# Layer 0's gated MLP rewritten: four batches wide, the weights stationary, every product as three float32r products on split halves, the down products issued two tiles later

## The chip, the cores and the metric

One core of a Trainium2 chip runs the whole program. The metric is the device time in microseconds, the median of several executions. PE is the matrix engine (PEld its weight loads), DVE the vector engine, ACT the scalar engine, POOL the general one, SP the engine that issues the DMAs.

## What is computed

Two decoder layers on x of 16 batches x 128 tokens x 256, each with self attention, cross attention and a gated MLP, each behind a layernorm. The change lies in the MLP of layer 0:

```python
def _mlp(x, gw, uw, dw):
    g = x @ gw.T
    u = x @ uw.T
    return g * jax.nn.sigmoid(g) * u @ dw.T
logits = x @ router_weight.T                      # 8 experts
topk_vals, topk_idx = jax.lax.top_k(logits, 2)
comb_w = jnp.sum(jax.nn.softmax(topk_vals) * (topk_idx < 8), axis=-1)
shared = _mlp(x, sh_gate, sh_up, sh_down)         # inner width 1024
routed = _mlp(x, r_gate, r_up, r_down)            # inner width 128
x = x_in + shared + routed * comb_w[:, None]      # x here is layernorm(x_in)
```

## The kernel before

x stays in SBUF for the whole program, 128 tokens on the partitions, 256 columns per batch. The program is a chain of blocks, one per sublayer, and each block has one instruction stream per engine, written out by hand and tied by semaphores; no scheduler moves anything. All engines finish a block before the next begins. Each block loads the next one's weights by DMA.

`gated_mlp` is the block in question. It takes one batch per turn in a software pipeline (`pipeline`: four steps written out, then a loop of two). For batch t: DVE normalises x into h (`dve_normalise`), PE transposes h (`pe_transpose_h`), ACT copies it out of PSUM (`act_copy_hT`), and PE multiplies. The activations are the moving side with 128 columns (one batch) and the weights the stationary side, in plain f32 (L1629). The three parts of a batch are the routed expert with the router (L1639) and two halves of four inner tiles. For each part ACT computes tanh(g/2) (L1545), DVE forms (tanh+1) * g (L1570) and multiplies by u (L1575). In the next turn PE multiplies by the down weights (L1617, L1621), here with the inner activations stationary and 256 weight columns moving. DVE then adds both results to x (L1594, L1596) and takes the statistics for the next layernorm (`dve_statistics`, L169 to L173); POOL raises the variance to the power -1/2 (`pool_rstd`, L134).

The first cross attention (`normed_cross_attention`) already multiplies in float32r: a value is split in a high part (its float32r rounding) and a low part (the rest), and three products of the parts (`PARTS`: high x high, high x low, low x high) stand for one f32 product.

## Time and profile before

| | |
|---|---|
| median of 3 runs | 1830.47 us (1828.85 to 1833.53) |
| the profiled execution, its own time | 1829.69 us |
| its span, first to last instruction | 1827.7 us |
| busy: PE, DVE, ACT, POOL | 92%, 62%, 42%, 38% of the span |
| mean granted clock of PE | 0.979 of full speed |
| the gated MLP's block, by its instructions | about 702 to 910 us |

An engine is busy where one of its instructions runs. Idle time matters on the engine that bounds a stage, and there the profile names what ended it. [...]

### The profile page before, as it was taken

What the parts mean: (1) busy time and instruction counts of PE and PEld (TensorE: products, weight loads), DVE (VectorE), ACT (ScalarE), POOL (GpSimd) and SP (SyncE); (2) the same over time, 40 slices, a digit from 0 to 9 for tenths busy, and PEclk for the clock granted to TensorE, in tenths of its full rate; (3) what the DMA queues carried; (4) which work ended last, traced back from release to release, by engine and by line L of the source; (5) the groups of instructions that cost most, each with busy time, mean ns of one, the idle gap of its engine ahead of it and who ended that gap; (6) DMA issues with size and microseconds to landing.
All of it is one profiled execution on the core that took longest, in us unless ns stands there. A gap on an engine that the chain in (4) does not pass through costs nothing. (4 is left out here: it accounts for less than half of the span.)

```text
span 1827.7 us, 33438 instructions
## 1 busy us (share of the span) xinstructions
PE 1681.9 (92%) x10800; PEld 1283.1 (70%) x10800; DVE 1129.3 (62%) x2543; ACT 771.2 (42%) x1771; POOL 691.5 (38%) x884
## 2 busy tenths in 40 slices
PE   4999889999999998999878888899999999888887
PEld 2555568888888887999845555588888888644444
DVE  3666557677676663554445666445556555499996
ACT  1444346767676762111134444344444444311111
POOL 3666535454545541000012222023333322366665
PEclk9999989999999999999979999999999999999999
DMA  5000020000000000000020000200000000000000
GB/s 210 1 0 0 1 81 4 3 3 3 1 3 3 1 2 20 1 0 0 2 114 0 0 0 0 76 6 7 6 6 6 6 3 5 0 7 10 10 9 11
DMA packets 15631, 28.41 MB, mean 16 GB/s; under 512 B 1745, under 2 KB 12242, under 8 KB 14802
## 3 DMA queue, kind: packets, MB, share of 16 engines
q1 hardware_dynamic: 15570, 27.63, 4.1%
q8 instruction: 34, 0.56, 0.1%
q14 instruction: 27, 0.22, 0.0%
HBM read 25.53 MB, written 2.10 MB: 15 GB/s over the span
## 5 line engine op out<-in xcount | busy, mean ns | idle before, releaser
L1237 POOL TENSOR_TENSOR weights_even<-weights_even,cross_reciprocal 128x512 f32<-128x512 f32 x64 | 66.7, 1043 | 283.2 <-DVE cross_reciprocal L1341 283.2
L134 POOL TENSOR_TENSOR rstd<-variance,minus_half 128x1 f32 (+1 forms) x80 | 43.9, 549 | 336.1 <-DVE variance L173 336.1
L844 POOL TENSOR_TENSOR weights_odd<-weights_odd,cross_reciprocal 128x512 f32<-128x512 f32 x64 | 66.5, 1040 | 191.6 <-DVE cross_reciprocal L970 191.6
L1629 PE MATMUL bank<-mlp_hT,weights_even 128*128 128x128 f32 x1152 | 136.5, 278 | 0.5 <-ACT mlp_hT L152 0.5
L1629 PEld LDWEIGHTS bank<-mlp_hT,weights_even 128*128 128x128 f32 x1152 | 133.6, 193 | 1.5 <-ACT mlp_hT L152 0.8
L1420 PE MATMUL bank<-cross_hT,cross_wqk 128*128 128x128 f32 x1024 | 124.9, 275 | 0.6 <-ACT cross_hT L1267 0.6
L1033 PEld LDWEIGHTS bank<-ident,weights_odd 128*128 128x128 f32 x768 | 94.1, 141 | 44.4 <-issue 32.4
L1101 PE MATMUL bank<-weights_odd 128*128 128x256 f32 x512 | 121.5, 380 | 1.6 <-ACT weights_odd L900 1.6
L1453 PE MATMUL bank<-weights_even 128*128 128x256 f32 x512 | 121.2, 380 | 0.7 <-ACT weights_even L1291 0.7
L1420 PEld LDWEIGHTS bank<-cross_hT,cross_wqk 128*128 128x128 f32 x1024 | 119.5, 192 | 0.9 <-ACT cross_hT L1267 0.9
L1033 PE MATMUL bank<-ident,weights_odd 128*128 128x128 f32 x768 | 115.5, 273 | 2.2 <-DVE weights_odd L956 2.2
L1848 DVE TENSOR_REDUCE grouped_maxima<-bank 128x4 bf16<-128x512 f32 x128 | 82.3, 685 | 56.5 <-PE bank L1914 56.4
L2216 PE MATMUL bank<-weights_even,mx_hT 128*128 128x512 f32 x256 | 115.2, 593 | 1.1 <-ACT mx_hT L152 1.1
L1279 ACT ACTIVATE weights_even<-bank,cross_shift 128x128 f32<-128x128 f32 x256 | 73.0, 368 | 74.3 <-DVE cross_shift L1331 73.7
L1762 ACT ACTIVATE grouped_probs<-bank 128x512 f32<-128x512 f32 x128 | 67.6, 600 | 85.9 <-PE bank L1932 85.9
L1101 PEld LDWEIGHTS bank<-weights_odd 128*128 128x128 f32 x512 | 92.3, 190 | 13.6 <-ACT weights_odd L900 3.5
L1453 PEld LDWEIGHTS bank<-weights_even 128*128 128x128 f32 x512 | 92.3, 190 | 11.4 <-ACT weights_even L1291 1.5
L883 ACT ACTIVATE weights_odd<-bank,cross_shift,cross_q_rms 128x128 f32<-128x128 f32 x256 | 95.9, 457 | 2.6 <-DVE cross_shift L950 2.6
L1329 DVE TENSOR_REDUCE cross_maxima<-bank 128x4 f32<-128x512 f32 x64 | 44.2, 691 | 78.7 <-PE bank L1430 78.6
L1336 DVE TENSOR_REDUCE cross_sums<-weights_even 128x4 f32<-128x512 f32 x64 | 43.9, 686 | 77.3 <-ACT weights_even L1279 77.3
L368 POOL TENSOR_TENSOR causal_masked_maxima<-causal_maxima,causal_constants 128x512 bf16<-128x512 bf16 x64 | 67.7, 1079 | 60.6 <-DVE causal_maxima L493 60.6
L1047 PE MATMUL bank<-high_weights,cross_high 128*128 128x512 f32 x192 | 87.5, 456 | 1.2 <-DVE cross_low L979 1.2
(264 smaller groups left out, 4029.7 us busy)
## 6 DMA issues: line engine op xcount, KB each, us to landing
weights_odd<-in_weights SPq DMA_DIRECT2D x2, 3072.0 KB, 14.0
weights_even<-in_weights SPq DMA_DIRECT2D x2, 2560.0 KB, 11.7
weights_even<-in_weights SPq DMA_DIRECT2D x2, 1732.0 KB, 8.7
weights_odd<-in_weights SPq DMA_DIRECT2D x2, 1536.0 KB, 8.7
x<-in_x SPq DMA_DIRECT2D x4, 512.0 KB, 7.1
cross_context<-in_context SPq DMA_DIRECT2D x32, 64.0 KB, 1.8
out<-mx_result SPq DMA_DIRECT2D x16, 128.0 KB, 1.7
weights_even<-in_weights SPq DMA_DIRECT2D x2, 512.0 KB, 9.0
```

The lines of the kernel that those rows point to most:

```text
L368: pool.tensor_tensor(masked_maxima[g][:, :, :], maxima[s][:, g, :].unsqueeze(2).to_broadcast([P, PER, P]), later.unsqueeze(1).to_broadcast ...
L883: last = act.activation(probs[x][:, j, :], bank_scores[:, j * P:(j + 1) * P], ACT.Exp, scale=q_rms[x][:, j:j + 1], bias=shift[x][:, j:j + 1])
L1033: last = pe.transpose(bank[:, j * P:(j + 1) * P], source, core.ident[:, :])
L1047: last = pe.matmul(out, half[:, c, :], split_weights[b][:, at:at + PER * D], start=(k == 0), stop=(k == len(jobs) - 1))
L1101: last = pe.matmul(bank_y[:, 0:EMBED], headsT[x][:, j, :], wo[:, h, :], start=(h == 0), stop=(h == HEADS - 1))
L1279: last = act.activation(probs[x][:, j, :], bank_scores[x][:, j * P:(j + 1) * P], ACT.Exp, scale=SCALE, bias=shift[x][:, j:j + 1])
L1420: last = pe.matmul(bank_q[:, j * P:(j + 1) * P], wqk[:, c, h * D:(h + 1) * D], hT[s][:, c, :], start=(c == 0), stop=(c == EC - 1))
L1453: last = pe.matmul(bank_y[s][:, 0:EMBED], headsT[x][:, j, :], wo[:, h, :], start=(h == 0), stop=(h == HEADS - 1))
L1629: last = pe.matmul(out, wt[:, c, m * P:(m + 1) * P], layer.hT[:, c, :], start=(c == 0), stop=(c == EC - 1))
L1762: act.activation(probs[:, SLOTS * c + j, :], bank_scoresT[j][:, :], ACT.Exp, scale=SCALE)\
L1848: dve.tensor_reduce(maxima[s][:, g * PER:(g + 1) * PER], bank_scores[j].rearrange("p (h k) -> p h k", h=PER), AX.X, ALU.max).then_inc(max_ ...
L2216: last = pe.matmul(bank[:, :], layer.hT[:, c, :], wt[:, c, j * 512:(j + 1) * 512], start=(c == 0), stop=(c == EC - 1))
```

## The change

`gated_mlp` now takes a quad, four batches (512 token columns), at a time. The routed expert is tile 0 of nine inner tiles of 128; per tile the packed weights hold gate, up and down side by side (`by_inner_tile` on the host), and the router's 16 columns come last. All products are float32r: ACT writes the high parts of the weights, of h transposed and of the inner activations, DVE the low parts of the weights and of h, POOL the low part of the inner activations. Gate and up have the weights stationary and 512 columns moving, in two pairs of banks that alternate. Down has the inner activations of one batch stationary and 256 weight columns moving; the downs of a tile are issued behind the gate and up of the tile two later, or behind the quad's last tile. The whole block is written out, without a loop. The odd weight area, 12288 columns wide, exists only up to the cross attention; a new one of 6144 columns serves the blocks from `gated_mlp` on. The cut diff (the removed code is that of the functions above):

```diff
-    HALVES = 2
-    PER = TILES // HALVES
+    INTER, EXPERTS = 1024, 8
+    TILES = INTER // P + 1
+    QUAD = 4
+    QUADS = BATCHES // QUAD
+    LAST = TILES - 1
+    PER_TILE = 2 * EC * P + EMBED
+    ROUTER_AT = TILES * PER_TILE
+    COLUMNS = ROUTER_AT + EC * EXPERTS
...
+        split_weights = [sbuf(f"{name}_weights", [P, COLUMNS], F32R) for name in ("high", "low")]
+        h = sbuf("all_h", [P, QUAD, EMBED])
+        hT = [sbuf(f"{name}_hT", [P, EC, QUAD * P], F32R) for name in ("high", "low")]
...
+        halves = [[sbuf(f"{name}_inner{s}", [P, QUAD * P], F32R) for name in ("high", "low")] for s in range(2)]
...
+        bank_h, bank_y = core.banks[0:2], core.banks[6:8]
+        bank_gate, bank_up = [core.banks[2], core.banks[4]], [core.banks[3], core.banks[5]]
...
+            def low_inner(i):
+                pool.wait_ge(inner_high, i + 1)
+                pool.wait_ge(tile_down, downs(i - 2))
+                pool.tensor_tensor(halves[i % 2][1][:, :], inner[i % 2][:, :],
+                                   halves[i % 2][0][:, :].bitcast(F32), ALU.subtract).then_inc(inner_low, 1)
+
+            for q in range(QUADS + 1):
+                for k in range(TILES):
+                    if q < QUADS:
+                        low_inner(TILES * q + k)
+                    if q > 0 and 3 <= k < 3 + QUAD:
+                        layer.pool_rstd(pool, QUAD * (q - 1) + k - 3, STATISTICS_STEPS)
...
-            pipeline(act, step)
+            def high_weights(k):
+                act.activation(of_tile(split_weights[0], k), of_tile(region, k), ACT.Copy).then_inc(weights_high, 1)
+            act.activation(router_of(split_weights[0]), router_of(region), ACT.Copy)
+            high_weights(0)
+            high_weights(1)
+
+            def high_h(q):
+                for c in range(EC):
+                    act.wait_ge(layer.hT_filled, EC * q + c + 1)
+                    act.wait_ge(tile_filled, TILES * q)
+                    act.activation(hT[0][:, c, :], bank_h[c][:, :], ACT.Copy).then_inc(high_ready, 1)
+
...
+            def high_inner(i):
+                act.wait_ge(inner_ready, i + 1)
+                act.wait_ge(tile_down, downs(i - 2))
+                act.wait_ge(inner_low, nonneg(i - 1))
+                act.activation(halves[i % 2][0][:, :], inner[i % 2][:, :], ACT.Copy).then_inc(inner_high, 1)
...
+            high_h(0)
+            for q in range(QUADS):
+                for k in range(TILES):
+                    i = TILES * q + k
+                    if i > 0:
+                        high_inner(i - 1)
+                    tanh_of_gate(i)
+                    if k == 1:
+                        exponent(q)
+                    if q == 0 and k + 2 < TILES:
+                        high_weights(k + 2)
+                if q + 1 < QUADS:
+                    high_h(q + 1)
+            high_inner(TILES * QUADS - 1)
...
-            pipeline(dve, step)
+            def low_weights(k):
+                dve.wait_ge(weights_high, k + 1)
+                dve.tensor_tensor(of_tile(split_weights[1], k), of_tile(region, k),
+                                  of_tile(split_weights[0], k).bitcast(F32), ALU.subtract).then_inc(weights_low, 1)
+
...
+            def low_h(q):
+                for c in range(EC):
+                    dve.wait_ge(high_ready, EC * q + c + 1)
+                    dve.tensor_tensor(hT[1][:, c, :], bank_h[c][:, :], hT[0][:, c, :].bitcast(F32), ALU.subtract)\
+                       .then_inc(low_ready, 1)
+
+            def gate(i):
+                dve.wait_ge(tanh_ready, i + 1)
+                dve.wait_ge(inner_ready, nonneg(i - 1))
+                dve.scalar_tensor_tensor(gated[i % 2][:, :], tanh[i % 2][:, :], 1.0, bank_gate[i % 2][:, :],
+                                         ALU.add, ALU.mult).then_inc(gated_ready, 1)
+                dve.wait_ge(gated_ready, i + 1)
+                dve.wait_ge(inner_high, nonneg(i - 1))
+                dve.wait_ge(inner_low, nonneg(i - 1))
+                dve.tensor_tensor(inner[i % 2][:, :], gated[i % 2][:, :], bank_up[i % 2][:, :], ALU.mult)\
+                   .then_inc(inner_ready, 1)
...
+                dve.wait_ge(tile_down, downs(TILES * q))
+                dve.wait_ge(layer.x_updated, QUAD * q)
...
+            def update_x(q, j):
+                b = QUAD * q + j
+                dve.wait_ge(tile_down, DOWN_STEPS * q + LAST + j // 2 * 2 + 2)
+                dve.wait_ge(routed_added, b + 1)
+                dve.scalar_tensor_tensor(layer.new_x[:, :], y_of(bank_y, j), 0.5, x_routed[:, j, :],
+                                         ALU.mult, ALU.add).then_inc(layer.x_updated, 1)
+                dve.wait_ge(layer.x_updated, b + 1)
+                tail_step.start(b)
+                layer.dve_statistics(dve, b, tail_step)
+
+            for j in range(QUAD):
+                normalise(0, j)
+            dve.wait_ge(weights_high, 1)
+            dve.tensor_tensor(router_of(split_weights[1]), router_of(region), router_of(split_weights[0]).bitcast(F32),
+                              ALU.subtract)
+            low_weights(0)
+            low_h(0)
+            low_weights(1)
+            for q in range(QUADS):
+                for k in range(TILES):
+                    gate(TILES * q + k)
...
+                        best_two(q)
+                    if k == 1:
+                        shares(q)
+                    if q > 0 and k in (1, 2):
+                        update_x(q - 1, 2 * k - 2)
+                        update_x(q - 1, 2 * k - 1)
+                    if k == 3:
+                        add_routed(q)
+                    if q + 1 < QUADS and 4 <= k < 4 + QUAD:
+                        normalise(q + 1, k - 4)
+                    if q == 0 and k + 2 < TILES:
+                        low_weights(k + 2)
+                if q + 1 < QUADS:
+                    low_h(q + 1)
+            for j in range(QUAD):
+                update_x(QUADS - 1, j)
...
-            pipeline(pe, step)
+            def turn_h(q):
+                pe.wait_ge(layer.h_ready, QUAD * (q + 1))
+                pe.wait_ge(routed_added, QUAD * q)
+                for c in range(EC):
+                    for j in range(QUAD):
+                        last = pe.transpose(bank_h[c][:, j * P:(j + 1) * P], h[:, j, c * P:(c + 1) * P],
+                                            core.ident[:, :])
+                    last.then_inc(layer.hT_filled, 1)
+
+            def route(q):
+                pe.wait_ge(low_ready, EC * (q + 1))
+                pe.wait_ge(weights_low, 1)
...
+                for j in range(QUAD):
+                    for m, (c, a, b) in enumerate(jobs):
+                        at = ROUTER_AT + c * EXPERTS
+                        last = pe.matmul(bank_h[0][:, j * EXPERTS:(j + 1) * EXPERTS], hT[a][:, c, j * P:(j + 1) * P],
+                                         split_weights[b][:, at:at + EXPERTS],
+                                         start=(m == 0), stop=(m == len(jobs) - 1))
+                last.then_inc(logits_filled, 1)
+
+            def gate_and_up(i, k):
+                if i < TILES:
+                    pe.wait_ge(weights_low, k + 1)
+                pe.wait_ge(inner_ready, nonneg(i - 1))
+                jobs = [(c, a, b) for c in range(EC) for a, b in PARTS]
+                for which, bank in enumerate((bank_gate[i % 2], bank_up[i % 2])):
+                    for m, (c, a, b) in enumerate(jobs):
+                        at = k * PER_TILE + (which * EC + c) * P
+                        last = pe.matmul(bank[:, :], split_weights[b][:, at:at + P], hT[a][:, c, :],
+                                         start=(m == 0), stop=(m == len(jobs) - 1))
+                last.then_inc(tile_filled, 1)
+
+            def down(q, k):
+                i = TILES * q + k
+                at = k * PER_TILE + 2 * EC * P
+                pe.wait_ge(inner_low, i + 1)
+                if k == 0:
+                    pe.wait_ge(top_ready, q + 1)
+                if k == 1:
+                    pe.wait_ge(layer.x_updated, QUAD * q)
+                for j in range(QUAD):
+                    for m, (a, b) in enumerate(PARTS):
+                        if k == 0:
+                            start, stop = m == 0, m == len(PARTS) - 1
                         else:
+                            start, stop = k == 1 and m == 0 and j % 2 == 0, k == LAST and m == len(PARTS) - 1
+                        last = pe.matmul(y_of(bank_h if k == 0 else bank_y, j),
+                                         halves[i % 2][a][:, j * P:(j + 1) * P], split_weights[b][:, at:at + EMBED],
+                                         start=start, stop=stop, skip_group_check=(k > 0))
+                    if k == LAST or j == QUAD - 1:
+                        last.then_inc(tile_down, 1)
+
+            turn_h(0)
+            for q in range(QUADS):
+                route(q)
+                for k in range(TILES):
+                    gate_and_up(TILES * q + k, k)
+                    if q > 0 and k == 0:
+                        down(q - 1, LAST)
+                    if k >= 2 and k < LAST:
+                        down(q, k - 2)
+                if q + 1 < QUADS:
+                    turn_h(q + 1)
+                down(q, LAST - 2)
+                down(q, LAST - 1)
+            down(QUADS - 1, LAST)
```

The instruction order around a quad's end, on PE. Before, one step of the pipeline (layer_even_9 is `inner_ready`, layer_even_11 `gap_ready`, layer_even_2 `hT_ready`, layer_even_0 `h_ready`):

```order
L146 MATMUL bank0<-ident,mlp_h 128x128 [waits layer_even_0]
L146 MATMUL bank0<-ident,mlp_h 128x128
...
L1617 MATMUL bank6<-weights_even,mlp_inner 128x256 [waits layer_even_9]
...
L1621 MATMUL bank6<-weights_even,mlp_inner 128x256 [waits layer_even_9]
L1621 MATMUL bank6<-weights_even,mlp_inner 128x256 x3
...
L1629 MATMUL bank5<-mlp_hT,weights_even 128x128 [waits layer_even_9,layer_even_11,layer_even_2]
L1629 MATMUL bank5<-mlp_hT,weights_even 128x128 x3
L1639 MATMUL bank5<-weights_even,mlp_hT 128x8 x2
L1629 MATMUL bank1<-mlp_hT,weights_even 128x128 [waits layer_even_9]
```

Now (layer_even_20 is `inner_low`, layer_even_7 `weights_low`, layer_even_9 `low_ready`, layer_even_22 `routed_added`):

```order
L1731 MATMUL bank<-mlp_low_hT,mlp_high_weights 128x512
L1707 MATMUL bank<-ident,mlp_all_h 128x128 [waits layer_even_22,layer_even_0]
L1707 MATMUL bank<-ident,mlp_all_h 128x128 x7
L1749 MATMUL bank<-mlp_high_weights,mlp_high_inner 128x256 [waits layer_even_20]
L1749 MATMUL bank<-mlp_low_weights,mlp_high_inner 128x256
L1749 MATMUL bank<-mlp_high_weights,mlp_low_inner 128x256
...
L1718 MATMUL bank<-mlp_high_weights,mlp_high_hT 128x8 [waits layer_even_7,layer_even_9]
L1718 MATMUL bank<-mlp_low_weights,mlp_high_hT 128x8
L1718 MATMUL bank<-mlp_high_weights,mlp_low_hT 128x8
...
L1731 MATMUL bank<-mlp_high_hT,mlp_high_weights 128x512 [waits layer_even_18]
```

Transposes were two per step with a batch's downs behind them; now eight stand between the last gate and up tile and two tiles of downs (24 products), then 24 router products, then the next quad's first tile.

DVE around the update of x. Before, within the loop's step:

```order
L1592 SCALAR_TENSOR_TENSOR mlp_router<-mlp_router 128x1
...
L1594 SCALAR_TENSOR_TENSOR mlp_x_routed<-bank,mlp_router,x 128x256
...
L1596 SCALAR_TENSOR_TENSOR mlp_new_x<-bank,mlp_x_routed 128x256
L169 BN_STATS mlp_stats<-mlp_new_x 128x6
...
L173 TENSOR_SCALAR variance<-mlp_mean_var 128x1
...
L1570 SCALAR_TENSOR_TENSOR mlp_gated<-mlp_tanh,bank 128x128
```

Now, tiles 1 and 2 of a quad after the first:

```order
L1626 SCALAR_TENSOR_TENSOR mlp_gated<-mlp_tanh,bank 128x512
L1631 TENSOR_TENSOR mlp_inner<-mlp_gated,bank 128x512
L1649 TENSOR_SCALAR mlp_router<-mlp_router 128x4
...
L1665 SCALAR_TENSOR_TENSOR mlp_new_x<-bank,mlp_x_routed 128x256
...
L172 TENSOR_SCALAR variance<-mlp_mean_var 128x1
L1665 SCALAR_TENSOR_TENSOR mlp_new_x<-bank,mlp_x_routed 128x256
...
L172 TENSOR_SCALAR variance<-mlp_mean_var 128x1
L1626 SCALAR_TENSOR_TENSOR mlp_gated<-mlp_tanh,bank 128x512
L1631 TENSOR_TENSOR mlp_inner<-mlp_gated,bank 128x512
L1665 SCALAR_TENSOR_TENSOR mlp_new_x<-bank,mlp_x_routed 128x256
```

One update stood in each step; now two stand behind the gate of tile 1 and two behind that of tile 2, all of the quad before.

## Rows read from the trace of the kernel before

**Rows 1.** Page: busy time of PE, and the granted clock in 40 slices.

```profile
PE 1681.9 (92%) x10800; PEld 1283.1 (70%) x10800; DVE 1129.3 (62%) x2543; ACT 771.2 (42%) x1771; POOL 691.5 (38%) x884
...
PEclk9999989999999999999979999999999999999999
```

**Rows 2.** Busy time by stretch (PE, PEld, DVE, ACT, POOL; clock; DMA).

```profile
700.00:712.00 12.00, 9.19 (x66) 8.98 (x67) 3.12 (x12) 1.46 (x4) 0.56 (x1) 0.86 0.23 72
712.00:890.00 178.00, 178.00 (x1356) 169.69 (x1355) 89.33 (x268) 27.30 (x70) 7.68 (x14) 1.00 0.00 0
```

**Rows 3.** Waits, 700 to 912 us: total, times, longest.

```profile
ACT mlp_tanh L1545 <- PE bank L1639: 70.5, 16, 4.6
...
PEld bank L1621 <- DVE mlp_inner L1575: 3.1, 16, 0.4
```

**Rows 4.** Groups by form, 700 to 912 us: busy us, mean ns, idle before.

```profile
L1629 PE MATMUL bank<-mlp_hT,weights_even 128*128 128x128 f32 x1152 | 136.5, 278 | 0.5 <-ACT mlp_hT L152 0.5
...
L1621 PE MATMUL bank<-weights_even,mlp_inner 128*128 128x256 f32 x256 | 58.9, 382 | 0.0
...
L1570 DVE SCALAR_TENSOR_TENSOR mlp_gated<-mlp_tanh,bank 128x512 f32<-128x512 f32 x32 | 22.0, 688 | 57.2 <-ACT mlp_tanh L1545 57.2
...
L1545 ACT ACTIVATE mlp_tanh<-bank 128x512 f32<-128x512 f32 x32 | 19.1, 597 | 61.3 <-PE bank L1629 61.3
...
L1596 DVE SCALAR_TENSOR_TENSOR mlp_new_x<-bank,mlp_x_routed 128x256 f32<-128x256 f32 x16 | 6.8, 424 | 0.6
...
L139 DVE TENSOR_SCALAR mlp_h<-x,mean,rstd 128x256 f32 x12 | 4.9, 407 | 0.0
```

**Rows 5.** Timeline, one batch of the steady part: start, us, engine, line.

```profile
768.85 0.53 PEld L1639 LDWEIGHTS bank<-weights_even,mlp_hT 128*128 128x128 f32 x4
...
769.30 7.23 PEld L1629 LDWEIGHTS bank<-mlp_hT,weights_even 128*128 128x128 f32 x64
...
781.46 0.53 PEld L1639 LDWEIGHTS bank<-weights_even,mlp_hT 128*128 128x128 f32 x4
```

**Rows 6.** Timeline of PE in the first cross attention (float32r).

```profile
508.42 0.60 PE L1033 MATMUL bank<-ident,weights_odd 128*128 128x128 f32 x4
508.77 0.48 PE L1047 MATMUL bank<-high_weights,cross_high 128*128 128x512 f32 x1
...
510.26 1.02 PE L1092 MATMUL bank<-weights_odd,cross_context 128*128 128x512 f32 x2
```

**Rows 7.** Busy time and granted clock by half microseconds, stage start.

```profile
703.50:704.00 0.50, 0.50 (x4) 0.50 (x4) 0.00 (x0) 0.00 (x0) 0.00 (x0) 0.51 0.70 286
...
707.00:707.50 0.50, 0.50 (x6) 0.50 (x6) 0.06 (x1) 0.20 (x1) 0.00 (x0) 1.00 0.00 0
```

**Rows 8.** Timeline, PE's first work in the stage.

```profile
702.28 0.41 PE L146 MATMUL bank<-ident,mlp_h 128*128 128x128 f32 x2 [3.13 <-DVE mlp_h L139]
...
704.64 0.97 PEld L1639 LDWEIGHTS bank<-weights_even,mlp_hT 128*128 128x128 f32 x4
...
705.50 6.68 PEld L1629 LDWEIGHTS bank<-mlp_hT,weights_even 128*128 128x128 f32 x53
```

**Rows 9.** Timeline of DVE, last batch of the stage.

```profile
908.59 0.42 DVE L1596 SCALAR_TENSOR_TENSOR mlp_new_x<-bank,mlp_x_routed 128x256 f32<-128x256 f32 x1
909.05 0.43 DVE L169 BATCH_NORM_STATS2 mlp_stats<-mlp_new_x 128x6 f32<-128x256 f32 x1
...
910.00 0.14 DVE L173 TENSOR_SCALAR variance<-mlp_mean_var 128x1 f32<-128x1 f32 x1
```

**Rows 10.** Timelines, first cross attention: DVE's normalise, POOL beside it.

```profile
505.45 0.74 DVE L139 TENSOR_SCALAR cross_h<-x,mean,rstd 128x256 f32 x1
...
505.00 1.04 POOL L844 TENSOR_TENSOR weights_odd<-weights_odd,cross_reciprocal 128x512 f32<-128x512 f32 x1 [3.06 <-DVE cross_reciprocal L970]
```

**Rows 11.** The next stage: clock, 949 to 952 us, and PE there.

```profile
949.00:952.00 3.00, 1.99 (x11) 1.23 (x12) 1.51 (x6) 0.95 (x2) 0.00 (x0) 0.54 0.00 0
...
950.01 1.11 PE L1971 MATMUL bank<-ident,grouped_outT 128*128 128x128 f32 x4 [1.97 <-ACT grouped_outT L1796]
```

212 lines of the change are left out of this document (76 added, 136 removed).

## The prediction, made before the change was run

> **What bounds the kernel now.** I read the page first. TensorE's matmuls fill 92% of the span, and its clock is at full speed nearly everywhere [rows 1]. The stage that the change rewrites is the gated MLP of layer 0, about 702 to 910 us. The busy time of each engine by stretch shows it: in the 178 us from 712 to 890 PE is busy for all 178, weight loads for 170, DVE for half, ACT for 15%, POOL for 4% [rows 2]. The waits say the same: ACT waits 70.5 us for PE's router products alone, PE's weight loads wait for DVE 3.1 us in all [rows 3]. So this stage costs what PE's work costs, and a batch takes 781.46 - 768.85 = 12.61 us, from the router's loads of one to those of the next [rows 5], the stage 16 times that plus its edges. Its last DVE instruction (the variance of batch 15) ends at 910.00 + 0.14 = 910.14 [rows 9]. Nothing outside the stage changes but the address of one weight area; the next stage starts behind the block's end, so what this stage saves or loses comes off the end one to one.
>
> **PE's price before and after.** A plain f32 product shows as two records. A record of 128 columns takes 136.5 / 1152 = 0.118 us in the mean [rows 4] and 7.23 / 64 = 0.113 in the steady part [rows 5], one of 256 columns 58.9 / 256 = 0.230 [rows 4]. Float32r shows in the cross attention: six products of 512 columns from 508.77 to 510.26, one record each, 0.248; without the first, which follows transposes, 0.234 [rows 6]. So the gate and up tile of four batches costs 12 x 0.234 = 2.8 us. Before, the same work is 4 batches x 4 products (gate and up, two halves of the contraction) x 2 records x 0.113 = 3.6 us. Three float32r products replace one f32 product and cost 0.78 of it.
>
> The down product is float32r with **256** columns and a fresh 128x128 load each time, and no row shows that. Lower bound: a weight load with almost no product behind it (8 columns) comes every (769.30 - 768.85) / 4 = 0.112 us [rows 5]. Upper bound: a whole 512-column product, 0.234. Nearest row: an f32 record of 128 columns streams its columns more than once (0.230 for 256 is twice 0.113 for 128, while float32r does 512 in 0.234), so it is as much streaming as 256 float32r columns, also with a load each, and takes 0.113. I take half of the 512-column price, 0.117. A tile of downs is then 12 x 0.117 = 1.4 us, against 4 x 2 x 0.230 = 1.84 before.
> [...]
>
> New work on PE: the router, 24 products of 8 columns per quad with a load each, 24 x 0.112 = 2.7 us. Transposes: four in 0.35 us [rows 6], so eight and the switch 0.8.
> A full quad: 9 x 2.8 + 9 x 1.4 + 2.7 + 0.8 = 41.3 us, against 4 x 12.61 = 50.4. If PE alone counted, four quads would save 36 us.
>
> **What lies on the path besides.** Prices: ACT 512 columns 0.60, DVE 512 columns 0.69 and 256 columns 0.42 [rows 4], POOL 512 columns 1.04 [rows 10]. From fill to fill: tanh starts 0.3 us after PE's last issue, ends at 0.9, gated and inner until 2.4, the high half until 3.1, POOL's low half until 4.3. In steady state the downs of a tile are issued two tiles later, 7 us: covered. DVE's 1.4, ACT's 1.2 and POOL's 1.04 per 4.2 us tile are covered too.
>
> (a) Quad boundary. After the last gate/up tile PE has eight transposes and two tiles of downs, 3.6 us. DVE must first do gate of tile 8 (to 2.4), then both low halves of h (2 x 0.69), 3.9 to 4.0. Then only can the router start: **0.4 us** wait.
>
> (b) Update of x. `down(q, 1)` overwrites the y banks and waits for all four `new_x` of the quad before. From the end of gate/up tile 0, PE needs 1.4 + 2.8 (until tile 1 is filled), then 2.8 + 1.4 + 2.8 = 7.0 to reach that wait. DVE, once tile 1 is filled, needs 1.0 for tanh and signals, gate 1.4, the shares 0.65, two updates, gate 1.4, one update and the `new_x` of the fourth. One update from `new_x` to variance is 910.14 - 908.59 = 1.55, and two chained instructions follow with 0.04 between [rows 9]: period 1.6. Sum 1.0 + 1.4 + 0.65 + 3.2 + 1.4 + 1.6 + 0.45 = 9.7; 9.7 - 7.0 = 2.7 us. Behind `down(q,1)` stands all of PE. To this comes POOL's low half: a 128x256 normalise that takes 0.41 with POOL idle [rows 4] takes 0.74 beside a POOL instruction of 1.04 us that began before it [rows 10]. The copy of x in each update has the same form, and POOL works twice in that stretch. Each copy can wait up to some 0.8 of such an instruction, or miss it: bounds 2.7 and 4.3. I add 0.6: **3.3 us** in each of three quads.
> [...]
>
> (c) Start. Before, the first transposes run at 702.28 [rows 8]. Now four normalises come first, 3 x 0.41: 703.5. The clock falls to 0.51 at 703.5, as before [rows 7]. Eight transposes at about 0.18: 704.9; high half 0.2 + 0.6, low half 0.7 and signals: 706.6. ACT's and DVE's split of the first two weight tiles (128x768; half as much again as 512 columns, 0.9 and 1.0 us) lies beside this. The router at half clock: four loads took 705.50 - 704.64 [rows 8], 0.215 each, so 24 take 5.2: 711.8. The first gate/up tile partly at half clock, 3.7: 715.5.
> (d) Quad 0. 8 x 2.8 + 8 x 1.4 + 0.8 = 34.4. Tile 2 waits for DVE to have done gate 0, the four maxima and one low weight tile (2.4 + 0.9 + 1.0, signal 0.2 = 4.5, against 2.8): 1.7. End 751.6. The other weight splits fit into the 4.2 us per tile.
> (e) Three quads: 3 x (41.3 + 0.4 + 3.3) - 0.8 (no transposes after the last) = 134.2: 885.8.
> (f) Tail. The last gate/up tile ended 2.8 earlier, 883.0; its low half is there 4.4 later, 887.4; half of the last downs and signal 0.9; four updates on DVE alone 3 x 1.6 + 1.55: **894.6**. Before, one update stood there; now four do.
>
> So without the clock the stage ends 15.5 us earlier.
> (g) **Clock.** After an idle of 3.13 us [rows 8] the grant fell to 0.51 and came back to 1.00 at 707.0, 3.5 us later [rows 7]. At 949 to 952 it fell after a wait of only 1.97 us [rows 11]. Each fall costs half of what runs in it, 3.4 / 2 = 1.7 us. Six places invite it: three waits (b) of 3.3 us and three routers, where PE streams 8 columns at a time after a wait. I take three falls: 5.1 us (bounds none and six with one double length, 12).
>
> Sum: 15.5 - 5.1 = 10.4 us faster. Against the profiled execution's own time, 1829.69 us (span 1827.7), that is 1819.3; it stands 0.8 under the median of the runs shown, 1830.47, so I forecast **1820** for the median.
>
> **The rivals.**
> A, slower: float32r at 256 columns costs as much as at 512 (load exposed, or the columns streamed at half rate). 432 x 0.117 = 50 us more on PE, about 6 of it absorbed by the waits in (b): about 1864. For it: no row of this form. Against: the f32 records, whose loads hide behind as much streaming. It decides from 0.117 + 10.4 / 432 = 0.141 us a product.
> B, within noise or slower: the clock falls at every boundary and wait and stays down longer, as rows 11 show that a short wait can be enough. Six falls of 3.4 us cost 10 (1825), of double length 20 (1835). Against: the page's PEclk stands at 9 in all slices but one [rows 1].
> [...]
> C, faster: no falls, waits at 2.7, downs at 0.112, the router counted as work for the clock at the start. 5.1 + 1.8 + 2.2 + 1.6: 1809.
> D, that the wide form does nothing because something else bounds: per quad DVE has 9 x 1.4 + 4 x 1.6 + 10 x 0.45 + 2 x 0.69 = 25 us, ACT 20 x 0.6 = 12, POOL 9 x 1.04 = 9, against PE's 41. Excluded but for the places (a) and (b).
>
> **Numbers.** Likeliest 0.66, its own range 1814 to 1826 (0.06 of it within 0.3%). A 0.06, B 0.16 (0.02 faster, 0.07 within, 0.07 slower), C 0.12. 1809 to 1832 holds about 8 in 10. 0.3% is 5.5 us, about what a measurement of this kernel tells from no change. Faster 0.60 + 0.12 + 0.02 = 0.74, same 0.06 + 0.07 = 0.13, slower 0.06 + 0.07 = 0.13.
>
> **What the new profile shows.** Downs near 0.117 us a record; PE waiting for DVE's `new_x` at `down(q,1)` about 3.3 us in three places; a short wait for `low_hT` at the router; PEclk under 1.00 at some of these; stage end near 900 instead of 910. I am wrong if the downs' price is above 0.14, or if the granted clock in the stage is far under 0.96.

## The result and the profile after

The changed kernel takes **1821.55 us** in the median (1817.94 to 1827.40, 10 runs), the kernel before 1830.88 (1828.85 to 1833.95, 10 runs). The ratio is 0.9945, 95% interval 0.9933 to 0.9957: 9 us faster, with 1820 forecast. The profiled execution took 1818.1 (span 1816.3); it is the second shortest of the ten.

The page first, engines and granted clock, as in [rows 1]:
```profile
span 1816.3 us, 32069 instructions
PE 1652.9 (91%) x10256; PEld 1244.5 (69%) x10256; DVE 1132.9 (62%) x2489; ACT 796.4 (44%) x1785; POOL 740.8 (41%) x920
PEclk9999989999999998999889999899999999999999
```
PE is busy for less and POOL has work in this stage, but PEclk has 8s now in slices 16 (681 to 726 us), 20 (863 to 908) and 26, where it had 9s. Slices 21 (an 8 where it had a 7) and 26 lie behind the stage, and so does part of 20. The groups of PE from 697 to 905 us, keeping shapes apart (line, engine, operation, tiles, shape, count; busy us, mean ns; idle before and its releasers):
```profile
L1731 PE MATMUL bank<-mlp_high_hT,mlp_high_weights 128*128 128x512 f32 x144 | 59.4, 412 | 0.7 <-DVE mlp_low_weights L1608 0.7
...
L1749 PE MATMUL bank<-mlp_high_weights,mlp_high_inner 128*128 128x256 f32 x144 | 42.4, 294 | 12.4 <-DVE mlp_new_x L1665 11.1 <-POOL mlp_low_inner L1544 1.3
```
A record overlaps the next one (its length, 0.28 us, is more than the distance to it), so the price is read from start to start. In the timeline of PE (start, length), at the end of downs and in the gate and up tile behind them:
```profile
742.12 0.28 PE L1749 MATMUL bank<-mlp_high_weights,mlp_low_inner 128*128 128x256 f32 x1
...
742.59 0.40 PE L1731 MATMUL bank<-mlp_high_hT,mlp_high_weights 128*128 128x512 f32 x1
...
745.16 0.40 PE L1731 MATMUL bank<-mlp_low_hT,mlp_high_weights 128*128 128x512 f32 x1
745.40 1.03 PE L1707 MATMUL bank<-ident,mlp_all_h 128*128 128x128 f32 x8
746.19 0.36 PE L1749 MATMUL bank<-mlp_high_weights,mlp_high_inner 128*128 128x256 f32 x1
```
A float32r product of 256 columns with a fresh load comes every 0.118 us ((742.59 - 742.12) / 4), one of 512 every 0.234 ((745.40 - 742.59) / 12), eight transposes take 0.79. Rival A, which had 0.234 for the first as well, is out. In the following rows the 24 router products run from 749.10 to 751.70: 0.108 each.

The waits of PE from 697 to 905 us (total, times, longest):
```profile
PE bank L1749 <- DVE mlp_new_x L1665: 11.1, 3, 3.7
PE bank L1707 <- DVE mlp_all_h L1614: 4.0, 1, 4.0
PE bank L1718 <- DVE mlp_low_hT L1620: 1.6, 1, 1.6
PE bank L1749 <- POOL mlp_low_inner L1544: 1.3, 1, 1.3
PE bank L1731 <- DVE mlp_low_weights L1608: 0.7, 1, 0.7
```
The first row is the forecast wait (b), 3 x 3.7. What DVE did ahead of it in quad 1, and PE behind it (timeline, with the wait in brackets):
```profile
762.01 0.43 DVE L168 BATCH_NORM_STATS2 mlp_stats<-mlp_new_x 128x6 f32<-128x256 f32 x1
762.47 0.74 DVE L169 TENSOR_SCALAR x<-mlp_new_x 128x256 f32<-128x256 f32 x1
...
764.50 0.29 DVE L169 TENSOR_SCALAR x<-mlp_new_x 128x256 f32<-128x256 f32 x1
...
767.41 1.32 DVE L169 TENSOR_SCALAR x<-mlp_new_x 128x256 f32<-128x256 f32 x1
...
769.11 0.42 DVE L1665 SCALAR_TENSOR_TENSOR mlp_new_x<-bank,mlp_x_routed 128x256 f32<-128x256 f32 x1
761.77 1.29 POOL L1544 TENSOR_TENSOR mlp_low_inner<-mlp_inner,mlp_high_inner 128x512 fp32r<-128x512 f32 x1 [2.95 <-ACT mlp_high_inner L1579]
767.32 1.27 POOL L1544 TENSOR_TENSOR mlp_low_inner<-mlp_inner,mlp_high_inner 128x512 fp32r<-128x512 f32 x1 [4.26 <-ACT mlp_high_inner L1579]
769.68 0.36 PE L1749 MATMUL bank<-mlp_high_weights,mlp_high_inner 128*128 128x256 f32 x1 [3.71 <-DVE mlp_new_x L1665]
```
The copy of x takes 0.29 us by itself, but 0.74 and 1.32 when POOL's low half runs; it ends 0.15 after POOL's instruction does (763.21 and 763.06, 768.73 and 768.59). The statistics (0.43), which read the same tile, kept their time beside POOL.

The clock behind that wait, by the microsecond (window; length; PE, PEld, DVE, ACT, POOL busy with counts; granted clock; DMA):
```profile
769.00:770.00 1.00, 0.32 (x3) 0.35 (x4) 0.93 (x4) 0.00 (x0) 0.00 (x0) 1.00 0.00 0
770.00:771.00 1.00, 1.00 (x10) 1.00 (x9) 0.90 (x5) 0.00 (x0) 0.00 (x0) 0.82 0.00 0
771.00:772.00 1.00, 1.00 (x5) 0.92 (x5) 0.96 (x2) 0.00 (x0) 0.00 (x0) 0.50 0.00 0
773.00:774.00 1.00, 1.00 (x4) 0.81 (x3) 0.67 (x2) 0.00 (x0) 1.00 (x1) 0.50 0.00 0
774.00:775.00 1.00, 1.00 (x5) 0.81 (x5) 0.00 (x0) 0.00 (x0) 0.63 (x2) 0.97 0.00 0
815.00:816.00 1.00, 0.00 (x0) 0.00 (x0) 0.97 (x4) 0.00 (x0) 0.62 (x1) 0.51 0.00 0
821.00:822.00 1.00, 1.00 (x4) 0.77 (x4) 0.00 (x0) 0.00 (x0) 1.00 (x2) 0.58 0.00 0
822.00:823.00 1.00, 1.00 (x6) 0.83 (x5) 0.00 (x0) 0.00 (x0) 0.19 (x1) 1.00 0.00 0
```
There is one fall (a stretch at clock 0.50) at each wait (b) and none at a router. The first begins 0.9 us behind the end of the wait (at 770.6) and lasts 3.4 us; the second (815.0 to 821.8) and the third (862.8 to 869.6) begin while PE still waits and last 6.8, of which PE works for 5.

**Where the time came from.** I measure the stage from the POOL `rstd` of the last cross batch to the last variance. Its start, in the timelines of POOL before and after:
```profile
700.82 0.56 POOL L134 TENSOR_TENSOR rstd<-variance,minus_half 128x1 f32<-128x1 f32 x1 [7.08 <-DVE variance L173]
698.69 0.56 POOL L133 TENSOR_TENSOR rstd<-variance,minus_half 128x1 f32<-128x1 f32 x1 [7.08 <-DVE variance L172]
```
Before, it is 700.82 to 910.14, 209.3 us [rows 9]. Its end after, in DVE's timeline:
```profile
899.49 0.15 DVE L171 TENSOR_SCALAR mean<-mlp_mean_var 128x1 f32<-128x1 f32 x1
899.56 0.14 DVE L172 TENSOR_SCALAR variance<-mlp_mean_var 128x1 f32<-128x1 f32 x1
```
The second line is the last variance, so the stage is 698.69 to 899.70, 201.0 us: **8.3 us** of the 11.4 between the two profiled spans. The stage began 2.1 earlier (unchanged code ahead of it) and what follows took 1.0 less.

### The profile page after: what moved, and what is told of

Read it like the earlier page. It is cut to its first block and busy times, and to the rows that moved or that the text cites. A ratio compares the mean times of both kernels' runs of the same rounds, so it can differ in the third digit from the quotient of the medians.

```text
span 1816.3 us, 32069 instructions
## 1 busy us (share of the span) xinstructions
PE 1652.9 (91%) x10256; PEld 1244.5 (69%) x10256; DVE 1132.9 (62%) x2489; ACT 796.4 (44%) x1785; POOL 740.8 (41%) x920
## 5 line engine op out<-in xcount | busy, mean ns | idle before, releaser
L843 POOL TENSOR_TENSOR weights_odd_early<-weights_odd_early,cross_reciprocal 128x512 f32<-128x512 f32 x64 | 66.7, 1042 | 191.7 <-DVE cross_reciprocal L969 191.7
L1032 PEld LDWEIGHTS bank<-ident,weights_odd_early 128*128 128x128 f32 x768 | 94.3, 141 | 44.2 <-issue 32.9
L1100 PE MATMUL bank<-weights_odd_early 128*128 128x256 f32 x512 | 121.5, 380 | 1.6 <-ACT weights_odd_early L899 1.6
L1032 PE MATMUL bank<-ident,weights_odd_early 128*128 128x128 f32 x768 | 115.8, 274 | 2.2 <-DVE weights_odd_early L955 2.2
L1544 POOL TENSOR_TENSOR mlp_low_inner<-mlp_inner,mlp_high_inner 128x512 fp32r<-128x512 f32 x36 | 48.3, 1342 | 138.6 <-ACT mlp_high_inner L1579 138.6
L1100 PEld LDWEIGHTS bank<-weights_odd_early 128*128 128x128 f32 x512 | 92.3, 190 | 13.5 <-ACT weights_odd_early L899 3.5
L1452 PEld LDWEIGHTS bank<-weights_even 128*128 128x128 f32 x512 | 92.3, 190 | 11.4 <-ACT weights_even L1290 1.5
L882 ACT ACTIVATE weights_odd_early<-bank,cross_shift,cross_q_rms 128x128 f32<-128x128 f32 x256 | 96.1, 458 | 2.6 <-DVE cross_shift L949 2.6
L1290 ACT ACTIVATE weights_even<-bank 128x512 f32<-128x512 f32 x64 | 38.3, 598 | 112.4 <-PE bank L1443 112.4
```

The costliest lines, as they stand in the source:

```text
L882: last = act.activation(probs[x][:, j, :], bank_scores[:, j * P:(j + 1) * P], ACT.Exp, scale=q_rms[x][:, j:j + 1], bias=shift[x][:, j:j + 1])
L1032: last = pe.transpose(bank[:, j * P:(j + 1) * P], source, core.ident[:, :])
L1100: last = pe.matmul(bank_y[:, 0:EMBED], headsT[x][:, j, :], wo[:, h, :], start=(h == 0), stop=(h == HEADS - 1))
L1452: last = pe.matmul(bank_y[s][:, 0:EMBED], headsT[x][:, j, :], wo[:, h, :], start=(h == 0), stop=(h == HEADS - 1))
```

## The experiments

These are twelve kernels, which undo or add one thing or combine such edits. Each ratio is against the kernel before, run beside it; "the stage" is the stretch just defined. The clock falls are read from one profiled execution of each kernel.

**e1: the four new_x first.** Theory: wait (b) is a matter of order on DVE, and the clock falls hang on it. Rivals: the falls are the router's; the wait only moves.
```
+ new_x = sbuf("four_new_x", [P, QUAD, EMBED])
  if q > 0 and k == 1:
+     for j in range(QUAD): update_x(q - 1, j)    # writes new_x only
  if q > 0 and k in (1, 2):
-     update_x(q - 1, 2 * k - 2); update_x(q - 1, 2 * k - 1)
+     statistics(q - 1, 2 * k - 2); statistics(q - 1, 2 * k - 1)    # statistics and copy of x
...
```


> The four new_x of a quad are written one after the other into a buffer of four when tile 1 of the next quad begins; statistics and copy of x follow where they stood, two batches at k=1 and two at k=2. Nothing else moves. Before it, PE waited three times for new_x, 11.1 us in all, the longest 3.7, and the clock fell behind each of these waits. My theory: a third and a fourth new_x no longer stand behind three statistics (3 x 1.6 us and more), so the wait is gone (four new_x take 4 x 0.45 = 1.8 us, over 5 us before PE comes there). The 11 us come off the end, and if the clock falls because of these waits, its three spells (3.4, 6.6 and 7.7 us at 0.5, so about 8 us lost) vanish too: 11 to 19 us faster than the kernel after, about 1803 to 1811. Rival 1: the spells come from the router's 8-column products, which stay: 11 us alone, with the granted clock of the stage as low as now (1810 to 1812). Rival 2: the wait only moves to another part of the chain on DVE (statistics and copies stand in the way of gate of tiles 1 and 2 as before, so that inner and its halves are late for a later down): less than 5 us faster, and a wait of PE for low_inner instead.


**1802.05 us** (1801.78 to 1804.51), ratio 0.9849 (0.9836 to 0.9863), 19.5 under the kernel after (17.6 by the two ratios); the stage 184.8, 16.2 shorter. No wait for new_x is left. In the same place as above PE goes straight on:
```profile
766.56 0.39 PE L1744 MATMUL bank<-mlp_low_hT,mlp_high_weights 128*128 128x512 f32 x1
766.79 0.28 PE L1762 MATMUL bank<-mlp_high_weights,mlp_high_inner 128*128 128x256 f32 x1
```
The three falls at the waits went too: the stage is shorter by 11.1 us of waits and by 5 of clock (6.7 that these falls cost, less 1.7 for a new one). The new fall (795.5 to 798.9) came 4 us behind the first product of a router, so rival 1 was not all wrong.

**e2: no copy.** Theory: the copies beside POOL make up 2.1 of the 3.7.
```
- dve.scalar_tensor_tensor(layer.new_x[:, :], y_of(bank_y, j), ...)
- dve.tensor_scalar(core.batch_x(b), layer.new_x[:, :], 1.0, None, ALU.mult)   # in the helper
+ dve.scalar_tensor_tensor(core.batch_x(b), y_of(bank_y, j), ...)
```


> new_x is written straight over x of its batch, and the copy of 256 columns by DVE is left out (16 copies, a mean of 570 ns each, between 290 and 1320). The order of all else stays. My theory: in the chain ahead of the wait stand three copies, of which those that run beside POOL's low half take 0.74 and 1.32 us instead of 0.29: the three waits of 3.7 fall to about 1.6 us each, 6 us in all, and in the tail four copies of 0.3 go, 1.2 us. With the clock falls as they are: 7 us faster than the kernel after, 1814 to 1815; if the shorter waits no longer bring the clock down, up to 8 us more, 1806. Rival: POOL only locks out whichever DVE instruction stands there next, so its 1.3 us are paid by another one: 3 x 3 x 0.3 + 1.2 = 4 us faster at most.


**1812.08** (1810.88 to 1812.75), ratio 0.9897 (0.9882 to 0.9912); the stage 195.1, 5.9 shorter. The wait is what the theory gave, 2.1 less (0.74 + 0.29 + 1.32 = 2.35, less some 0.08 by which the next instruction starts before each copy ends):
```profile
PE bank L1753 <- DVE x L1665: 4.9, 3, 1.6
```
The rival (another instruction pays) is out. What neither had: there is no clock fall at these waits, but one at each of the three quad boundaries, 2.2 to 3.5 us behind the router's first product. Two stretches of this kernel's clock, which hold a router each:
```profile
748.00:763.00 15.00, 15.00 (x83) 13.02 (x82) 4.36 (x15) 2.86 (x6) 2.57 (x2) 0.89 0.00 1
793.00:808.00 15.00, 15.00 (x75) 13.08 (x75) 2.94 (x10) 2.27 (x5) 2.57 (x2) 0.77 0.01 1
```

**e3: downs one tile later, not two.**
```
- if k >= 2 and k < LAST: down(q, k - 2)
+ if k >= 1: down(q, k - 1)
```


> The downs of a tile are issued one tile later instead of two. My theory: the chain from the end of a gate and up tile to its low half is about 4.3 us (tanh, gated, inner, high half, low half on three engines), and PE has 2.8 us of gate and up between. So each tile waits 1.5 us or a little more: the 4.2 us of a tile become 5.7, 32 tiles of 36 (about 50 us slower than the kernel after, 1870), before counting what the clock does in such waits (to 60 or more if it falls in many of them). Rival: in a steady state the chain overlaps anyway, and POOL, ACT and DVE catch up, so that the delay by two tiles is worth under 0.5 us a tile (under 18 us, 1822 to 1840).


**1850.70** (1849.35 to 1853.24), ratio 1.0115 (1.0098 to 1.0131), 29 to 31 us over the kernel after: between theory (50) and rival (under 18), and the theory's mechanism is wrong in the main. PE's waits from 697 to 912 us:
```profile
PE bank L1749 <- DVE mlp_new_x L1665: 19.0, 3, 6.3
PE bank L1718 <- DVE mlp_low_hT L1620: 6.1, 4, 1.6
PE bank L1749 <- POOL mlp_low_inner L1544: 2.3, 3, 1.8
```
The low half is late by 2.3 us in all (and by 2.5 once more in the tail, where the kernel after has 1.3), not by 1.5 a tile. The chain of 4.3 us was right, but I had set only gate and up (2.8) against it and left out the downs of the tile before (1.4), which PE issues first: 4.2. What grows is the wait for new_x (11.1 to 19.0), a 1.6 wait at each quad boundary, and the clock (six falls of 3.4 or 6.8 us ahead of the tail, one at each boundary and one in each wait for new_x).

**e4: the wide form in plain f32**, with no halves anywhere.
```
- jobs = [(c, a, b) for c in range(EC) for a, b in PARTS]
+ jobs = [(c, a, b) for c in range(EC) for a, b in ((0, 0),)]
- split_weights = [sbuf(f"{name}_weights", [P, COLUMNS], F32R) ...]
+ split_weights = [region, region]
```


> The wide form stays (four batches, weights as stationary side, downs two tiles later), but all its products are plain f32, so no value is split into high and low halves, on any engine. It tells the shape's share from that of float32r. From the rows: a plain product of 512 columns as two records of about 2 x 0.230, so 4 products a tile cost 4 x 0.92 = 3.7 us against 2.8, the downs 4 x 0.46 = 1.84 against 1.4, the router 16 records x 0.112 = 1.8 against 2.6, transposes 0.8: 52.4 us a quad against 41.3. My theory: all of the gain is the price of float32r, the shape by itself gains nothing: 4 x 11 = 44 us slower than the kernel after, less up to 20 us for waits and clock falls that a slower PE covers: 1845 to 1865, above the kernel before. Rival: the wide shape by itself gains (fewer weight loads, transposes in one piece): 1830 or less.


**1831.85** (1829.96 to 1834.09), ratio 1.0009 (0.9999 to 1.0019): the shape alone gains nothing, which was the theory; the size was off, 10 to 12 us over the kernel after where 24 to 44 was expected. In this kernel's timeline a gate and up tile starts at 733.65 and the next 5.16 us later, a record of 512 columns costs 0.43 (not 0.46), and a quad 50.0 us (806.89 - 756.89, a wait of 0.66 included) instead of 52.4. There is no fall of the clock from 714 to 911, and PE waits only 0.66 us for new_x, three times.

**e5: e1 and e2 together.**


> Both edits at once: the four new_x are written first, straight over x, and the copies are gone. With new_x first the waits were already gone (the run e1 waited for no new_x), so of the missing copies only the tail counts: after the last down four copies of 0.3 us stand on DVE ahead of the last variance, 1.2 us, and normalise for the next quad has more room, which nobody waits for. My theory: 1 to 1.5 us faster than e1, 1800 to 1801, but with the number of clock falls behind the 8-column router products open: they came once in three quad boundaries in e1 and three times in e2, each costing 1.7 to 2.8 us. If falls come behind every router as in e2: 1804 to 1806. Rival: without copies POOL's low half is delayed less and anything between gains more: under 1798.


**1803.49** (1802.11 to 1804.95), ratio 0.9856 (0.9840 to 0.9873): not told from e1, where the theory had 1 to 1.5 us less. The stage is 185.4 with one fall behind a router (837.7 to 841.1) and 13.7 us at half clock at the start.

**e6: e1 with the router behind tile 0** (and, at the start, its low weights split behind the low half of h).
```
- route(q)
  for k in range(TILES):
      gate_and_up(TILES * q + k, k)
+     if k == 0: route(q)
```


> On top of e1: the router of each quad is issued behind the gate and up tile 0 instead of ahead of it, and at the start its low weights are split behind low_h. At the start the router runs at half clock (24 products, 5.15 us instead of 2.6), and the clock rose 8.7 us after PE's first router product, in gate and up tile 0 (705.5 in the run before: one product earlier than the wait for low weights of tile 2). My theory: the start is a fixed stretch at half clock whatever runs in it, so the order changes nothing there, except that the wait for low_weights (0.7 us) goes; and if the clock at the boundaries falls because 8-column products follow a switch to transposes and downs, then with 512-column products just ahead it falls less: 1 to 4 us faster than e1 (1798 to 1801). Rival 1: the clock rises sooner when 512-column products run first, since the router's stretch hardly counts as work: at the start 2 to 3 us more. Rival 2: the gap of 8-column products between tile 0 and tile 1 brings the clock down just as often: 1802 as e1.


**1800.39** (1798.42 to 1806.33), ratio 0.9839 (0.9823 to 0.9855): not told from e1 either: 1798 to 1801 was the theory and 1802 rival 2, and the intervals overlap. In the profile falls came behind three of four routers (at 714, 755 and 800), each up to 4 us behind the first product of 8 columns. But the profiled execution is the longest of the five, 1806.3 us at a mean granted clock of 0.974; the other four took 1798.4 to 1803.5 at 0.978 to 0.980, where e1's five had 0.974 to 0.976. So rival 2 holds for this execution, and whether the later router often keeps the clock up stays open.

**e7: e2 with a router of 128 columns.** The same 24 products at the same places, but each streams 128 columns; the results of the other 120 are not read. Theory: the 8-column products bring the clock down.
```
+ routers = [sbuf(f"{name}_router", [P, EC, P], F32R) for name in ("high", "low")]
- pe.matmul(bank_h[0][:, j * EXPERTS:(j + 1) * EXPERTS], ..., split_weights[b][:, at:at + EXPERTS], ...)
+ pe.matmul(bank_h[0][:, j * P:(j + 1) * P], ..., routers[b][:, c, :], ...)
```


> On top of e2: each router product streams 128 columns instead of 8 (the 120 columns of other weights ahead of the router's are streamed with them and the results not read), 24 products as before, at the same places. In e2 the clock fell at all three quad boundaries, 2.6 to 3.4 us behind the router's first product, for 3.2, 5.7 and 3.9 us, and not behind the waits of 1.6 us. My theory: it is the products of 8 columns, during which the array does next to nothing, that bring it down. A product with a fresh load of 128 columns costs 0.112 at 8 columns and 0.118 at 256, so 128 columns cost the same 0.112 to 0.118, and with them the falls at the boundaries go: 6 us (half of 12.8) faster than e2, 1806. The start gains too, if the clock rises sooner: up to 2 us. Rival 1: the falls come from something else at the boundary (transposes, the 24 downs in a row, the switch of operands): same as e2, 1812. Rival 2: float32r with 128 columns costs more than with 256 (a price that no row shows): 96 products x 0.1 = 10 us slower.


**1809.05** (1807.61 to 1811.85), ratio 0.9891 (0.9873 to 0.9908), 3.0 under e2. The clock stays at 1.00 through all three boundaries; the stretches around the same routers as in e2:
```profile
750.00:765.00 15.00, 15.00 (x92) 13.26 (x91) 5.74 (x19) 3.15 (x6) 3.63 (x3) 1.00 0.00 1
793.00:808.00 15.00, 15.00 (x94) 13.36 (x93) 5.70 (x19) 3.31 (x7) 3.87 (x3) 1.00 0.01 1
```
PE issues 94 products in 15 us instead of 75. The stage is 187.9, 7.2 shorter than in e2; the median gives only 3.0 of it, and the two intervals overlap. In the two profiled executions, 4.7 apart, the other 2.4 were lost ahead of the stage, in code that is the same in both: the stage began at 697.6 in e2 and at 700.0 in e7. Products of 128 columns cost 0.11 each (750.26 to 752.89 for 24), so rival 2 is out; rival 1 (falls from something else at the boundary) is out by the clock in the stage, though not by the median. One of the three waits at `down(q, 1)` was now for the low half, 1.8 us.

**e8: all four edits.**


> All four edits: new_x first, no copy, router behind tile 0, router of 128 columns. My theory: e5 plus no clock fall between start and tail, plus what the later router gains at the start: PE's work for four quads at 41.1 us, 4.1 less than e2 with its waits. 1796 to 1799. Rival: the edits take away the same falls, so that it is as e5 or e6 alone: 1799 to 1802.


**1796.60** (1794.40 to 1800.63), ratio 0.9825 (0.9809 to 0.9842): the fastest, 33 under the kernel before and 22 (by the ratios) to 25 under the one after. The stage is 179.4, with 6.8 us at half clock at its start and then none until it ends:
```profile
702.00:708.00 6.00, 4.59 (x15) 3.61 (x15) 3.18 (x6) 1.43 (x3) 0.00 (x0) 0.50 0.33 131
709.00:870.00 161.00, 161.00 (x956) 142.03 (x955) 90.50 (x205) 51.82 (x88) 52.81 (x47) 1.00 0.00 1
```

**e9: the kernel after with the router of 128 columns alone.** Are the two causes separate?


> The kernel after with one change: each router product streams 128 columns instead of 8 (as in e7). In the kernel after the clock fell in each of the three waits for new_x (3.7 us) and at none of the routers. My theory: there are two causes, the waits and the 8-column products, and this takes away only the second. So the falls in the waits stay, as long as there (about 3.5 to 8 us each), and the time is that of the kernel after, 1820 to 1822; at most the start gains up to 2 us. Rival: the falls in the waits come only where a router of 8 columns ran some 20 us before, so that they go too: 8 us faster, 1813.


**1819.32** (1818.15 to 1822.86), ratio 0.9947 (0.9934 to 0.9961): the time of the kernel after. There are three waits of 3.7 again, and three falls of 3.4 us that begin 0.2 to 1.5 us behind their ends (the waits from 697 to 912 us; the clock around the first two, and between them with a router):
```profile
PE bank L1752 <- DVE mlp_new_x L1668: 11.1, 3, 3.7
770.00:775.00 5.00, 4.47 (x19) 4.12 (x20) 4.36 (x12) 0.63 (x1) 0.92 (x1) 0.66 0.00 0
777.00:813.00 36.00, 36.00 (x217) 31.90 (x217) 16.28 (x40) 9.83 (x18) 10.57 (x10) 1.00 0.00 1
818.00:823.00 5.00, 5.00 (x22) 4.28 (x21) 3.53 (x10) 0.63 (x1) 1.78 (x2) 0.66 0.00 0
```
The rival is out.

**e10: e4 with new_x first and no copy.**


> Plain f32 as in e4, with the four new_x first and no copies as in e5. In e4 PE waited 0.66 us three times for new_x and the clock fell nowhere between start and tail, so nothing is left on PE but its work: 50.0 us a quad. My theory: the waits' 2.0 us and 1.2 in the tail go, 1828 to 1829.5. Between this and e5 (1803.5) lies then what float32r is worth where PE has no waits: 25 us of the 34 that PE's work shrinks by (50.0 against 41.3 a quad, four times), the rest in clock falls and the start's splits. Rival: the order of DVE's work matters to f32 as little as nothing: 1831 to 1832.


**1827.16** (1826.44 to 1829.67), ratio 0.9988 (0.9978 to 0.9997), 4.7 under e4 (3.8 by the ratios) where 2.3 to 4 was expected. A quad takes 49.1 us (803.99 - 754.89) against 41.6 in e5 (792.37 - 750.77). With no waits on either side float32r is worth 1827.2 - 1803.5 = 24 us; between the kernel after and e4 it showed as 10 to 12.

**e11: e8 with downs one tile later.**


> The version with all four edits (e8, 1796.6), but with the downs of a tile one tile later instead of two. In e3 the delay by one cost 29 us, of which longer waits for new_x were 8 and clock falls some 8; with new_x first these two are gone. What is left is the chain of a tile itself: in e3 PE waited for the low half 0.1 to 0.2 us in most tiles, and 2 us at each quad boundary, where the downs of tile 8 stand behind the chain. My theory: 36 tiles x 0.15 + 4 x 2.5 = 12 to 17 us slower than e8, 1809 to 1814, falls of the clock at the boundaries included. Rival: all of the 29 us stay, since the chain is simply longer than 2.8 us: 1825.


**1810.50** (1806.69 to 1812.49), ratio 0.9887 (0.9872 to 0.9903), 11 (by the ratios) to 14 over e8, as the theory had it. PE waits 6.1 for low_hT at four quad starts (e8: 1.4 at one) and 5.0 for low_inner (1.3), and its clock falls at no boundary. So half or more of what the lag was worth in e3 (29 to 31 us) was the waits for new_x and the clock.

**e12: e8 with the router ahead of tile 0.**


> The version with all four edits without one: the router stands ahead of tile 0 again (so it is e5 with a router of 128 columns). My theory: with 128 columns no router brings the clock down, wherever it stands, so between the start and the tail PE's work is the same, 41.1 us a quad. At the start the low weights of tile 2 are waited for again, 0.7 us, and the clock stays down until 713, as in e7 and e9, instead of 708 as in e8 (it was 710 in e11, which starts the same as e8): 2 to 3 us. So 1798 to 1800, between e5 (1803.5) and e8 (1796.6). Rival: the router's place is what took the falls away together with its width: falls at boundaries again, and the time of e5, 1803.


**1802.50** (1800.26 to 1805.69), ratio 0.9856 (0.9843 to 0.9870): 2.5 over my theory's upper end, and not told from e5. Yet there is no fall behind any of its three later routers, so the rival's mechanism is out. The stage is 183.7, 4.2 more than in e8, nearly all of it in the start: 13.7 us at half clock against 6.8, half of which is 3.4 us, and the 0.7 wait for low weights:
```profile
702.00:715.00 13.00, 11.59 (x43) 10.22 (x43) 3.23 (x5) 1.48 (x3) 0.00 (x0) 0.50 0.15 57
716.00:872.00 156.00, 155.29 (x910) 136.29 (x909) 85.56 (x203) 50.82 (x87) 52.94 (x47) 1.00 0.00 1
```

## Why the prediction was right, and where its terms were off

The step on which it hung, the price of a 256-column float32r product, was right: 0.118 against 0.117, half of the 512-column price, with the f32 record of 128 columns (0.113) as the nearest row. A tile of gate and up took 2.81 (forecast 2.8), the transposes 0.79 (0.8), a router 2.60 (2.7). The mechanisms came as told: the wait of `down(q, 1)` for new_x three times, a fall of the clock in or just behind it three times, a start at half clock, a tail of four updates. The stage gained 8.3 us where the sum had 10.4. That it came so near is in part luck: (a) and (b) miss by 1.2 us in opposite directions, two parts of (c) by 0.8, and that three of the six places would fall was a choice that no row told. By its steps:

- **(a) quad boundary: 0.4 forecast, 0 measured.** The last down starts at 748.98 and the router at 749.10. DVE has both low halves of h done at 748.84, 3.4 us behind PE's last gate and up product where 3.9 to 4.0 was forecast, and PE itself takes 3.7. That is 1.2 us less in three quads.
- **(b) update of x: 3.3 forecast, 3.7 measured**, 1.2 more in three. The 2.7 without POOL in it was too high (e2: with no copy 1.6, and three copies of 0.29 give 2.5), and POOL's share too small: one copy met its instruction halfway (0.45 more) and one from the start (1.03 more), not 0.6 in all. POOL's own price was low, 1.29 instead of 1.04 [rows 10].
- **(c) start**: the first gate and up tile ends 14.7 us after `rstd`, as forecast, but the router starts 0.8 earlier than told (5.0 after `rstd`, not 5.8), and the tile behind it takes 4.6 instead of 3.7, since the clock is back only at 712.6, 3.8 us into the tile. **(d)** Until quad 0 is through it takes 35.7 instead of 36.1: the wait for low weights is 0.7, not 1.7, and PE's own work 0.6 longer.
- **(e)** from there to the last gate and up tile: 139.0 (749.10 to 888.08) against 131.4 + 5.1 of clock = 136.5. The 2.5 are 1.2 for (b), less 1.2 for (a), 1.6 of clock, and 0.9 of PE's own work: a quad without any wait is 41.6 (e5, e12), not 41.3.
- **(f) tail**: 11.6 as forecast.
- **(g) clock**: the number of falls was right, their length was not. I took 3.4 us for each, as in [rows 7]; two begin inside the wait and last 6.8. PE works for 3.4, 5.0 and 5.0 us in them, half of which is 6.7 instead of 5.1. That the falls belong to the waits, not to the routers, e9 and e1 show: with router products of 128 columns they stay, and without the waits they go. That routers can do it too, which rival B had, is shown by e2 and e7. The fall of [rows 11], which I put behind a wait of 1.97 us, begins at 949.3, while PE still waits until 950.0.

The forecast of 1820 then was 1.6 low, about the 2.1 that the stage fell short. (The profiled execution, 1818.1, came out under the forecast for it, 1819.3, because of the 3.1 us that its unchanged stretches took less than in the profile before.)

Rival D fell as forecast, but with an addition: a quad without waits is 49.1 us of PE's work in plain f32 (e10) and 41.6 in float32r (e5), 30 us in four quads, and between e4 and the kernel after only 10 to 12 reached the end. Wait (b) and its clock took 17.8 (11.1 + 6.7), and e1 got as much back. Of the 30 us, 24 show between e10 and e5. The other 6 are 3.0 in the start (e10 is only 4.5 behind e5 when router 1 starts, counted from `rstd`, not 7.5; e5 stood at half clock for 13.7 us there and e10 for 10.2), 1.7 in e5's one fall, and the rest in the last quad, whose tail takes 1.0 less in e10.

**What stays open.** Falls at quad boundaries behind a router of 8 float32r columns: 11 of 19 (profiles of after, e1, e2, e3, e5, e6), with 128 columns 0 of 17 (e7, e8, e9, e11, e12). That the width makes the difference is shown by the pair e2 and e7 above all. In e3, which gives three of the 11, each router also stood behind a wait of 1.6 us, and one of its falls began 0.8 us behind the router's first product; but e11 has waits of 1.6 us at the same three boundaries, there ahead of tile 0 with a router of 128 columns behind it, and no fall. Why one router of 8 columns brings the clock down and the next doesn't isn't shown. Each count is from one execution, and executions differ: the ten of the kernel after have mean granted clocks of 0.969 (1827.4 us) to 0.974. The plain f32 routers of e4 and e10 (16 records of 8 columns, 1.7 us) had no fall in 6, and whether that is their shortness or their form wasn't tried. Nor is it settled what makes the start's spell 6.8 us in e8 and 10.2 or 13.7 in the other changed kernels; e11 starts with the same instructions as e8 and had 10.2. So part of e8's lead over e12 may be luck of the spell's place: its five runs lie from 1794.4 to 1800.6, and the profiled one is the shortest, at a clock of 0.983 where the others had 0.977 to 0.981.

## What to carry to other kernels

When PE's products get cheaper, look for the wait that the slower products had covered, before counting the gain: here an unchanged order on DVE (new_x, statistics, copy, batch by batch) held `down(q, 1)` up by 3.7 us a quad, and writing the four values that PE waits for first was worth almost twice the whole rewrite. A wait of some 4 us on PE should be priced with the clock behind it, here about 0.6 of the wait on top (6.7 for 11.1), and a row of tiny products is better made wide where the columns cost nothing (e7's stage is 7.2 us shorter than e2's).

## What the runs showed of the hardware that I had not expected

- A float32r product with a fresh 128x128 load costs 0.108 us at 8 columns, 0.110 at 128, 0.118 at 256 and 0.234 at 512: up to 256 columns the price hardly moves with the columns.
- The longer the wait at `down(q, 1)`, the surer the fall of the clock: with 3.7 us in 6 of 6 (after, e9), beginning between 1.8 us before the end of the wait and 1.5 behind it; with 6.3 us in 3 of 3 (e3); but with 1.6 to 1.8 us in 0 of 6 (e2, e7) and with 0.66 in 0 of 3 (e4). This is no limit, since in the kernel before the next stage has a fall in a wait of 1.97 us [rows 11]. The clock fell also with PE busy all the time, behind the 8-column products (e2).
- A DVE copy of 128x256 from SBUF to SBUF takes 0.29 us by itself, 0.74 beside a POOL subtraction of 1.29 that began 0.70 before it, and 1.32 beside one of 1.27 that began 0.09 before it (762.47 and 761.77, 767.41 and 767.32 in the rows of the kernel after), while the statistics of the same tile kept their time (0.43) beside the first. Both slowed copies end 0.15 us behind POOL's instruction; what holds them up until then, no trace shows.
- POOL's subtraction that writes float32r takes 1.27 and 1.29 us for 128x512 in the rows above; the f32 product of [rows 10] takes 1.04.
